# One-hot blocks as a stream of 22 a quad in the last two edge passes of a four-layer graph network

## The chip, the cores and the metric

The kernel runs on one core of one Trainium2 chip. The metric is the device time in microseconds of one execution; the kernel before has a median of 4281.43 us over 3 runs (4277.96 to 4282.35).

## The reference

The reference is a stack of four graph layers on 6250 nodes with 96 features each and 106250 edges, sorted by target. Each layer reads a row of some table for every edge (by its source node), reduces the rows over the edges of a target, adds the result to the nodes and normalizes. Cut to the third and fourth layer, which the change touches:

```python
# third layer: ci, cj from the degrees
msg = feat[src] * ci[src, None]
agg = segment_sum(msg, dst, N) * cj[:, None]
h = where(in_deg[:, None] > 0, agg, feat)
x = layernorm(x + h @ weight + bias)
# fourth layer
h = x @ W
agg = segment_sum(h[src] * edge_weight[:, None], dst, N)
y = agg + bias;  y = layernorm(y) * gamma + beta
x = layernorm(x + y)
```

## The kernel before

The edges are cut into 832 tiles of 128 edges and 208 quads of four tiles. Four passes run over the quads, one for each layer, with the nodes' own work between them and beside them. The nodes are 49 tiles of 128 (NT), in 13 chunks of four (NC). The engines are programmed by hand, each with its own queue in program order, and wait for each other through semaphores that count quads.

In the third and fourth pass a quad `q` goes through these steps:

- GpSimd (POOL) issues one indirect DMA for each tile (line L630), which gathers 128 rows of the table `ci_table` (third pass) or `h_table` (fourth) into `rows[:, q % 4]`. It waits for `agg_done` of quad q - 4, since `rows` holds four quads.
- VectorE (DVE) makes the one-hot matrices `same` from the targets' ranks: in the third pass by one comparison of 128x512 (`one_hot`, L1348), in the fourth by four operations of 128x128 that compare and multiply with the edge weight (L1696). It waits for `agg_done` of quad q - 2.
- TensorE (PE) adds the rows into their targets' window by four products, `spread` (L908, matmuls at L728), and counts `agg_done`.
- ScalarE (ACT) adds the window into the sums `acc` (the helper `spread` of ACT, L1028 to L1032).

Some tiles are not gathered by GpSimd but fetched by a product with a one-hot matrix. In the kernel before these are the last tiles of 60 quads in each pass (`picked`: every third quad from 18 to 195). Such a tile needs 49 blocks, one for each node tile: VectorE compares the 128 source numbers with the node numbers of a block (`find`, L1588, after `away`, L1583), TensorE multiplies each block with the table in `near` and `far`, kept in SBUF as three bf16 parts (`fetch`, L925, 128x288), and VectorE adds up the three parts into `rows` (`take`, L1595). The 49 blocks of a tile are dealt over the three quads before its own as 16, 16 and 17; `found` holds one tile's 49 blocks. The table's parts are made at the start of the pass by `make_exact` (L1565 to L1572), one chunk a quad, from `stage`, which SyncE loads (L596).

Side work on the 49 node tiles goes with the first 49 quads of each of these passes. In the third pass ScalarE and TensorE do it (L1205, L950, L958). In the fourth VectorE writes `x_plus` at the end of its quad (L1705, counts `v_plus`), and ScalarE's first step in the quad (L1243) waits for `v_plus` of that quad and counts `v_done`. The last twelve quads (from 196, `TAIL * GQ`) are left without fetched tiles.

## Time and profile before

| | us |
|---|---|
| median of 3 runs | 4281.43 |
| the profiled execution, its own time | 4278.2 |
| its span in the trace | 4276.2 |
| third pass, first to last gather's start | 2305.2 to 3268.8 |
| fourth pass, first to last gather's start | 3288.5 to 4254.8 |
| granted TensorE clock, mean | 0.843 |

The span runs from the first to the last instruction. Engines work side by side, so busy times don't add up to it; what counts is which engine never waits for another. A granted clock of 1 is the upper of TensorE's two levels (2.4 GHz), 0.5 the lower (1.2 GHz).

### The profile page before, as it was taken

How to read it: one execution, taken by the hardware profiler on the slowest of the kernel's cores; microseconds unless marked ns; L12 is line 12 of the kernel's file. 1: busy time of each engine (PE TensorE's matmuls, PEld its weight loads, DVE VectorE, ACT ScalarE, POOL GpSimd, SP SyncE). 2: the span in 40 equal slices, each digit the busy share in tenths (PEclk: the TensorE clock that was granted, in tenths of full speed). 3: DMA queues.
4: the chain of work that ended last, by engine and by line, in shares of the span. 5: the costliest groups of instructions: out<-in, count | busy, mean ns of one | idle time of the engine just before them, and what ended most of it. 6: DMA issues, size and time to landing. Idle time of an engine off the chain costs nothing.

```text
span 4276.2 us, 68563 instructions
## 1 busy us (share of the span) xinstructions
PE 3037.4 (71%) x20922; PEld 2603.9 (61%) x20922; DVE 2905.5 (68%) x5203; ACT 1377.3 (32%) x4318; POOL 3094.2 (72%) x3246
## 2 busy tenths in 40 slices
PE   7777777777666766676683787667775567776776
PEld 6677777777656666666662565555554455555555
DVE  4666666666676666666666566666665687777777
ACT  2222222222444444444454332222223222222223
POOL 5677777777277777777757777777776777777776
PEclk7777878777689888888895898999986699999997
DMA  7776776676443333333322222222222222222222
GB/s 216 202 188 178 188 187 182 182 188 179 105 121 100 100 98 100 100 100 98 100 74 62 49 45 45 45 45 45 45 44 67 55 45 44 45 45 46 44 45 56
DMA packets 363802, 417.49 MB, mean 98 GB/s; under 512 B 225184, under 2 KB 277011, under 8 KB 363357
## 3 DMA queue, kind: packets, MB, share of 16 engines
q0 software_dynamic: 129280, 239.67, 23.0%
q1 hardware_dynamic: 234173, 173.44, 15.2%
q8 instruction: 186, 3.05, 0.3%
q14 instruction: 163, 1.34, 0.1%
HBM read 393.05 MB, written 19.77 MB: 97 GB/s over the span
## 4 chain that ended last, share of the span: by engine, by line
POOL 61%; issue 21%; PE 8%; DMA 4%; DVE 3%; ACT 1%; SPq 1%; ACTq 0%; DVEq 0%; POOLq 0%
POOL rows L630 60%; PE bank L728 3%; DMA rows<-kv_table,src_idx 2%; DMA rows<-pair_table,src_idx 1%; PE bank L934 1%; POOL acc_max L657 1%; PE bank L825 1%; SPq L448 0%; PE bank L741 0%; PE bank L742 0%; PE bank L773 0%; PE bank L682 0%; DVE prod L1417 0%; DVE score L1419 0%; DVE prod L1415 0%
## 5 line engine op out<-in xcount | busy, mean ns | idle before, releaser
L728 PE MATMUL bank<-same,rows 128*96 128x128 f32 x4992 | 766.3, 304 | 364.8 <-issue 208.7
L630 POOL DMA_INDIRECT rows<-kv_table,src_idx x832 | 793.7, 954 | 314.1 <-issue 272.4
L630 POOL DMA_INDIRECT rows<-pair_table,src_idx x832 | 787.9, 947 | 311.5 <-issue 247.7
L728 PEld LDWEIGHTS bank<-same,rows 128*96 128x96 f32 x4992 | 658.7, 184 | 469.0 <-issue 407.8
L1030 ACT COPY acc<-bank 96x511 f32 (+1 forms) x832 | 480.1, 577 | 1365.8 <-PE bank L728 1364.6
L630 POOL DMA_INDIRECT rows<-h_table,src_idx x772 | 732.3, 949 | 253.7 <-issue 235.0
L630 POOL DMA_INDIRECT rows<-ci_table,src_idx x772 | 729.6, 945 | 243.3 <-issue 234.7
L1588 DVE TENSOR_TENSOR spare<-bank,first_only 128x2048 bf16<-128x2048 f32 x360 | 838.2, 2328 | 17.6
L925 PE MATMUL bank<-acc_max,spare 128*128 128x288 bf16 x4320 | 655.8, 307 | 164.8 <-DVE spare L1588 164.4
L925 PEld LDWEIGHTS bank<-acc_max,spare 128*128 128x128 bf16 x4320 | 437.6, 104 | 320.8 <-DVE spare L1588 194.1
L728 PE MATMUL bank<-same,msg 128*105 128x128 f32 x1664 | 307.6, 344 | 219.8 <-ACT acc L1032 219.5
L1348 DVE TENSOR_TENSOR same<-bank,rank_col 128x512 f32<-128x512 f32 x624 | 420.5, 674 | 41.8 <-PE bank L728 41.8
L741 PE MATMUL bank<-weights,first_only 97*128 97x96 f32 x1664 | 397.2, 329 | 33.3 <-DMA first_only<-q_table 29.6
L728 PEld LDWEIGHTS bank<-same,msg 128*105 128x105 f32 x1664 | 264.4, 225 | 239.8 <-DVE same L1348 174.1
L1487 DVE TENSOR_TENSOR_SCAN first_only<-first_only,bank 96x512 f32<-96x512 bf16 x208 | 264.7, 1273 | 199.4 <-issue 166.6
L742 PE MATMUL bank<-first_only 128*128 128x96 f32 x1664 | 399.0, 330 | 0.0
L825 PE MATMUL bank<-ident,rows 128*96 128x128 f32 x832 | 148.3, 307 | 305.9 <-DMA rows<-pair_table,src_idx 305.3
L741 PEld LDWEIGHTS bank<-weights,first_only 97*128 97x128 f32 x1664 | 335.1, 249 | 35.7 <-issue 35.6
L1595 DVE TENSOR_REDUCE rows<-bank 128x96 f32<-128x288 f32 x120 | 54.9, 457 | 430.2 <-PE bank L925 430.2
L742 PEld LDWEIGHTS bank<-first_only 128*128 128x128 f32 x1664 | 330.7, 246 | 0.0
L1415 DVE TENSOR_TENSOR prod<-bank,rows 128x384 f32<-128x384 f32 x208 | 115.6, 556 | 300.1 <-DMA rows<-kv_table,src_idx 235.1
L825 PEld LDWEIGHTS bank<-ident,rows 128*96 128x96 f32 x832 | 95.1, 138 | 346.1 <-DMA rows<-pair_table,src_idx 339.9
(184 smaller groups left out, 4172.6 us busy)
## 6 DMA issues: line engine op xcount, KB each, us to landing
first_only<-in_attr_cols SPq DMA_DIRECT2D x104, 384.0 KB, 4.1
first_only<-q_table SPq DMA_DIRECT2D x832, 48.0 KB
first_only<-rank_rows SPq DMA_DIRECT2D x104, 256.0 KB
first_only<-keep_rows SPq DMA_DIRECT2D x104, 192.0 KB, 3.2
rows<-kv_table,src_idx POOLq DMA_INDIRECT x832
rows<-pair_table,src_idx POOLq DMA_INDIRECT x832
rows<-ci_table,src_idx POOLq DMA_INDIRECT x772
rows<-h_table,src_idx POOLq DMA_INDIRECT x772
```

The source lines that it names most:

```text
L630: pool.indirect_dma_start(rows[:, k, j, 0:width], None, table, bass.IndirectOffsetOnAxis(ap=src_idx[:, t:t + 1], axis=0)).then_inc(rows_in ...
L728: mm = pe.matmul(out[0:nrow, here], left(j), right(j), start=(j == 0), stop=(j == TQ - 1), skip_group_check=True)
L741: pe.matmul(quad(bank[k % 2], F)[:, j, :], attr[:, k, j * P:(j + 1) * P], w_e, start=True, stop=True)
L742: mm = pe.matmul(quad(bank[2 + k % 2], F)[:, j, :], pick[:, k % 2, j * P:(j + 1) * P], q_win[:, k, j, :], start=True, stop=True)
L825: tr = pe.transpose(bank[k % 2][0:F, j * P:(j + 1) * P], rows[:, k, j, F:PAIR], ident[:])
L925: mm = pe.matmul(bank[0][:, 0:PARTS * F], found[:, t, :], exact(t)[:, 0, :], start=(t == 0), stop=(t == NT - 1), skip_group_check=True)
L1030: act.copy(dst[0:nrow, bass.ds(first + 1, QE - 1)], src[0:nrow, 1:QE])
L1348: return dve.tensor_tensor(out, base, over(values[:, bass.ds(q * TQ, TQ)], n), ALU.is_equal)
L1415: dve.tensor_tensor(prod[:], quad(bank[2 + k % 2], F), rows[:, k, :, 0:F], ALU.mult).then_inc(prod_step, 1)
L1487: dve.tensor_tensor_scan(scanned[:, k % 2, :], keep_row[:, k, :], bank[k % 2][0:F, :], 0.0 if static(q) and q == 0 else scanned[:, (k - 1) ...
L1588: dve.tensor_tensor(found[:, lo:hi, :], away.rearrange("p (o e) -> p o e", o=1).to_broadcast([P, hi - lo, P]), over(hundreds[:, lo:hi], P) ...
L1595: dve.tensor_reduce(rows[:, k, TQ - 1, 0:F], bank[0][:, 0:PARTS * F].rearrange("p (m f) -> p f m", m=PARTS), AX_X, ALU.add).then_inc(fetch ...
```

## The change

Both passes fetch 84 tiles in place of 60. The blocks are no longer dealt by thirds of a tile: from quad 5 on every quad up to 195 makes and uses the next 22 blocks of one long stream, across the borders of tiles. A tile's quad is the second one after that of its last block, so the fetched tiles lie in quads two or three apart. A quad whose 22 blocks cross a border does two pieces of `find`, with a new `away` between them; `away` and the PSUM bank of the products alternate between two. The rule for reuse of `found` becomes: the blocks of quad q wait until TensorE has used those of quad q - 2. `stage` has four buffers in place of two, and two chunks go through `make_exact` in each of the quads 1 to 7.

In the fourth pass, up to quad 195, the edge weight leaves the one-hot matrices: VectorE makes them by the same single comparison as in the third pass, and ScalarE multiplies the rows by the weight in place (`weigh`, four operations of 128x96). TensorE's `spread` now waits for `weighted` and not for the gathers. ScalarE's addition of quad q - 1 stands behind `weigh` of quad q.

```diff
-    EVERY = 3
     PARTS = 3
-    START = NC + 2 + EVERY
-    picked = list(range(START, TAIL * GQ, EVERY))
-    piece_of = [NT * m // EVERY for m in range(EVERY + 1)]
+    BLOCKS = 22
+    BEGIN = 5
+
+    def last_turn(g):
+
+        return BEGIN + ((g + 1) * NT - 1) // BLOCKS
+
+    picked = [last_turn(g) + 2 for g in range(NQ) if last_turn(g) + 2 < TAIL * GQ]
     order_of = {q: g for g, q in enumerate(picked)}
-
-    def piece(q):
-
-        for m in range(EVERY):
-            g = order_of.get(q + EVERY - m)
-            if g is not None:
-                return g, m
-        return None
+    pieces = [[] for _ in range(NQ)]
+    for q in range(BEGIN, TAIL * GQ):
+        lo, hi = (q - BEGIN) * BLOCKS, min((q - BEGIN + 1) * BLOCKS, len(picked) * NT)
+        while lo < hi:
+            end = min(hi, (lo // NT + 1) * NT)
+            pieces[q].append((lo // NT, lo % NT, end - lo // NT * NT))
+            lo = end
+    assert all(2 * (q - 1) * CT + 2 * CT >= min(NT, (q - BEGIN + 1) * BLOCKS) for q in range(BEGIN, BEGIN + 3))
+
+    def pieces_before(q):
+
+        return sum(len(pieces[p]) for p in range(max(q, 0)))
+
+    def pieces_through(g):
+
+        return sum(of <= g for p in pieces for of, _, _ in p)
...
-        stage = carve(2 * CT * F).rearrange("p (b t f) -> p b t f", b=2, t=CT)
+        stage = carve(4 * CT * F).rearrange("p (b t f) -> p b t f", b=4, t=CT)
...
-        away = bank[7][:, P:2 * P]
+        away = [bank[7][:, P:2 * P], bank[7][:, 256 + F:256 + F + P]]
...
-                wait(sp, staged, (n - 2) * NC + c - 1)
+                wait(sp, staged, (n - 2) * NC + c - 3)
                 m = len(tiles_of(c))
-                sp.dma_start(stage[:, c % 2, 0:m, :], rows_of(ci_table if n == 2 else h_table, c, 0, F)).then_inc(stage_in[c % 2].sem, 16)
+                sp.dma_start(stage[:, c % 4, 0:m, :], rows_of(ci_table if n == 2 else h_table, c, 0, F)).then_inc(stage_in[c % 4].sem, 16)
...
             def spread(s, q, i, k, at):
 
                 wait(pe, s.same_done, q + 1)
-                wait(pe, rows_in[k], arrivals(s.n, q))
-                if q in order_of:
-                    wait(pe, fetched, s.picks + order_of[q] + 1)
+                if s.n == 3 and q < TAIL * GQ:
+                    wait(pe, weighted, q + 1)
+                else:
+                    wait(pe, rows_in[k], arrivals(s.n, q))
+                    if q in order_of:
+                        wait(pe, fetched, s.picks + order_of[q] + 1)
                 wait(pe, s.copied, q - 1)
                 window(bank[2 + 2 * (k % 2)], F, at, lambda j: rows[:, k, j, 0:F], lambda j: same[:, k % 2, j, :]).then_inc(s.agg_done.sem, 1)
 
             def fetch(s, q):
 
-                at = piece(q)
-                if at is None:
-                    return
-                g, m = at
-                wait(pe, found_done, (s.picks + g) * EVERY + m + 1)
-                for t in range(piece_of[m], piece_of[m + 1]):
-                    mm = pe.matmul(bank[0][:, 0:PARTS * F], found[:, t, :], exact(t)[:, 0, :], start=(t == 0), stop=(t == NT - 1),
-                                   skip_group_check=True)
-                mm.then_inc(found_used.sem, 1)
+                n = s.pieces + pieces_before(q)
+                for g, lo, hi in pieces[q]:
+                    n += 1
+                    wait(pe, found_done, n)
+                    for t in range(lo, hi):
+                        mm = pe.matmul(bank[g % 2][:, 0:PARTS * F], found[:, t, :], exact(t)[:, 0, :], start=(t == 0), stop=(t == NT - 1),
+                                       skip_group_check=True)
+                    mm.then_inc(found_used.sem, 1)
...
+            def weigh(q, k):
+
+                wait(act, rows_in[k], arrivals(3, q))
+                if q in order_of:
+                    wait(act, fetched, s3.picks + order_of[q] + 1)
+                for j in range(TQ):
+                    at = q * TQ + j
+                    ins = act.mul(rows[:, k, j, 0:F], rows[:, k, j, 0:F], weight_col[:, at:at + 1])
+                ins.then_inc(weighted.sem, 1)
...
-                    spread(q, k, acc, F, bank[2 + 2 * (k % 2)], part_sum, s3.agg_done, s3.held, s3.copied)
+                    if q < TAIL * GQ:
+                        weigh(q, k)
+                    if 0 < q <= TAIL * GQ:
+                        spread3(q - 1, (k - 1) % GQ)
+                    if q >= TAIL * GQ:
+                        spread3(q, k)
...
             def find(s, q):
 
-                at = piece(q)
-                if at is None:
-                    return
-                g, m = at
-                if m == 0:
-                    wait(dve, src_in[g % 2], ((s.n - 2) * len(range(g % 2, len(picked), 2)) + g // 2 + 1) * 16)
-                    st.did(dve.tensor_scalar(away, src_row[:, g % 2, :], iota_col[:, 0:1], None, ALU.subtract))
-                    st.settle()
-                    dve.sem_inc(away_done.sem, 1)
-                lo, hi = piece_of[m], piece_of[m + 1]
-                wait(dve, found_used, (s.picks + g - 1) * EVERY + m + 1)
-                dve.tensor_tensor(found[:, lo:hi, :], away.rearrange("p (o e) -> p o e", o=1).to_broadcast([P, hi - lo, P]),
-                                  over(hundreds[:, lo:hi], P), ALU.is_equal).then_inc(found_done.sem, 1)
+                wait(dve, found_used, s.pieces + pieces_before(q - 1))
+                for g, lo, hi in pieces[q]:
+                    if lo == 0:
+                        wait(dve, src_in[g % 2], ((s.n - 2) * len(range(g % 2, len(picked), 2)) + g // 2 + 1) * 16)
+                        st.did(dve.tensor_scalar(away[g % 2], src_row[:, g % 2, :], iota_col[:, 0:1], None, ALU.subtract))
+                        st.settle()
+                        dve.sem_inc(away_done.sem, 1)
+                    dve.tensor_tensor(found[:, lo:hi, :], away[g % 2].rearrange("p (o e) -> p o e", o=1).to_broadcast([P, hi - lo, P]),
+                                      over(hundreds[:, lo:hi], P), ALU.is_equal).then_inc(found_done.sem, 1)
 
             def take(s, q, k):
 
-                n = s.picks + order_of[q]
-                wait(dve, found_used, (n + 1) * EVERY)
-                dve.tensor_reduce(rows[:, k, TQ - 1, 0:F], bank[0][:, 0:PARTS * F].rearrange("p (m f) -> p f m", m=PARTS), AX_X,
+                g = order_of[q]
+                wait(dve, found_used, s.pieces + pieces_through(g))
+                dve.tensor_reduce(rows[:, k, TQ - 1, 0:F], bank[g % 2][:, 0:PARTS * F].rearrange("p (m f) -> p f m", m=PARTS), AX_X,
                                   ALU.add).then_inc(fetched.sem, 1)
+
+            def make_two(s, q):
+
+                for c in (2 * q - 2, 2 * q - 1):
+                    if 0 <= c < NC:
+                        make_exact(s, c)
...
-                    for j in range(TQ):
-                        at = bass.ds(q * TQ + j, 1)
-                        ins = dve.tensor_scalar(same[:, k % 2, j, :], iota_s[:], rank_col[:, at], weight_col[:, at], ALU.is_equal, ALU.mult)
+                    if q < TAIL * GQ:
+                        ins = one_hot(same[:, k % 2], iota_over, rank_col, q, P)
+                    else:
+                        for j in range(TQ):
+                            at = bass.ds(q * TQ + j, 1)
+                            ins = dve.tensor_scalar(same[:, k % 2, j, :], iota_s[:], rank_col[:, at], weight_col[:, at], ALU.is_equal, ALU.mult)
                     ins.then_inc(s3.same_done.sem, 1)
                     if q in order_of:
                         take(s3, q, k)
-                    if 0 < q <= NC:
-                        make_exact(s3, q - 1)
-                    find(s3, q)
+                    make_two(s3, q)
+                    if pieces[q]:
```

The next two pieces are VectorE's queue in the fourth pass, in quads with side work (two quads between 21 and 25 in each). `acc_max<-spare` at L1705 or L1745 is the write of `x_plus`. Before:

```order
L1696 TENSOR_SCALAR same<-iota_s,rank_col,src_hi 128x128 [waits agg_done]
L1696 TENSOR_SCALAR same<-iota_s,rank_col,src_hi 128x128 x3
L1588 TENSOR_TENSOR spare<-bank,first_only 128x2176 [waits exp_done]
L1705 SCALAR_TENSOR_TENSOR acc_max<-spare,r_all,bank 128x96 [waits v_done]
L1696 TENSOR_SCALAR same<-iota_s,rank_col,src_hi 128x128 [waits agg_done]
L1696 TENSOR_SCALAR same<-iota_s,rank_col,src_hi 128x128 x3
L1595 TENSOR_REDUCE rows<-bank 128x96 [waits exp_done]
L1583 TENSOR_SCALAR bank<-first_only,iota_col 128x128 [waits rank_in1]
L1588 TENSOR_TENSOR spare<-bank,first_only 128x2048 [waits seq,exp_done]
L1705 SCALAR_TENSOR_TENSOR acc_max<-spare,r_all,bank 128x96 [waits v_done]
```

After:

```order
L1383 TENSOR_TENSOR same<-bank,rank_col 128x512 [waits agg_done]
L1626 TENSOR_REDUCE rows<-bank 128x96 [waits exp_done]
L1619 TENSOR_TENSOR spare<-bank,first_only 128x2304 [waits exp_done]
L1616 TENSOR_SCALAR bank<-first_only,iota_col 128x128 [waits rank_in0]
L1619 TENSOR_TENSOR spare<-bank,first_only 128x512 [waits seq]
L1745 SCALAR_TENSOR_TENSOR acc_max<-spare,r_all,bank 128x96 [waits v_done]
L1383 TENSOR_TENSOR same<-bank,rank_col 128x512 [waits agg_done]
L1619 TENSOR_TENSOR spare<-bank,first_only 128x2816 [waits exp_done]
L1745 SCALAR_TENSOR_TENSOR acc_max<-spare,r_all,bank 128x96 [waits v_done]
```

The four operations that make `same` have become one, `find` writes 2816 columns (22 blocks) in place of 2048 or 2176, and one of the quads cuts its 22 blocks in two (2304 and 512) around a new `away`.

ScalarE's queue, one quad of the same stretch. `x_nodes<-acc_max` is its share of the side work, `rows<-rows` is `weigh`. Before:

```order
L1243 ACTIVATE x_nodes<-acc_max,s_all 128x96 [waits v_plus]
L1025 TENSOR_LOAD starts
L1028 ISA [waits copied]
L1028 ACTIVATE part_sum<-acc,cont 96x1
L1030 ISA [waits agg_done]
L1030 COPY acc<-bank 96x511
L1032 ACTIVATE acc<-bank,part_sum 96x1 [waits held]
```

After:

```order
L1272 ACTIVATE x_nodes<-acc_max,s_all 128x96 [waits v_plus]
L1248 ACTIVATE rows<-rows,src_hi 128x96 [waits prod_done,rows_in2]
L1248 ACTIVATE rows<-rows,src_hi 128x96 x3
L1041 TENSOR_LOAD starts
L1044 ISA [waits copied]
L1044 ACTIVATE part_sum<-acc,cont 96x1
L1046 ISA [waits agg_done]
L1046 COPY acc<-bank 96x511
L1048 ACTIVATE acc<-bank,part_sum 96x1 [waits held]
```

The scalings stand between the side work, which waits for `v_plus`, and the addition to `acc`.

TensorE's queue in the fourth pass, a little later (`same,rows` is `spread`, the 128x288 products are `fetch`). Before:

```order
L728 MATMUL bank<-same,rows 96x128 [waits copied,rows_in2,same_done]
L728 ISA
L728 MATMUL bank<-same,rows 96x128
L728 ISA
L728 MATMUL bank<-same,rows 96x128
L728 ISA
L728 MATMUL bank<-same,rows 96x128
L925 MATMUL bank<-acc_max,spare 128x288 [waits clip_done]
L925 MATMUL bank<-acc_max,spare 128x288 x3
L925 MATMUL bank<-first_only,spare 128x288 x13
```

After:

```order
L742 MATMUL bank<-same,rows 96x128 [waits copied,pick_done,same_done]
L742 ISA
L742 MATMUL bank<-same,rows 96x128
L742 ISA
L742 MATMUL bank<-same,rows 96x128
L742 ISA
L742 MATMUL bank<-same,rows 96x128
L941 MATMUL bank<-first_only,spare 128x288 [waits clip_done]
L941 MATMUL bank<-acc_max,spare 128x288 [waits clip_done]
L941 MATMUL bank<-acc_max,spare 128x288 x20
```

`spread` waits for `pick_done` (the semaphore behind `weighted`) where it waited for the rows, and 22 products follow it in two pieces, where 17 did.

## Rows read from the trace of the kernel before

**Rows 1.** The page: busy time of each engine, and the chain that ended last, by engine.

```profile
PE 3037.4 (71%) x20922; PEld 2603.9 (61%) x20922; DVE 2905.5 (68%) x5203; ACT 1377.3 (32%) x4318; POOL 3094.2 (72%) x3246
...
POOL 61%; issue 21%; PE 8%; DMA 4%; DVE 3%; ACT 1%; SPq 1%; ACTq 0%; DVEq 0%; POOLq 0%
```

**Rows 2.** The gathers line L630: duration min/median/max in ns, first and last start; what ended its idle time.

```profile
L630 POOL DMA_INDIRECT rows<-ci_table,src_idx x772: 940/944/1292, 2305.2 to 3268.8; - x193
...
L630 POOL DMA_INDIRECT rows<-h_table,src_idx x772: 940/944/1302, 3288.5 to 4254.8; - x193
...
  issue: 989.7, 3150
...
  PE bank L728: 5.8, 19
```

**Rows 3.** Stretches: length, then busy (count) of PE, PEld, DVE, ACT, POOL; clock; DMA.

```profile
2500.00:3100.00 600.00, 441.46 (x3217) 338.15 (x3218) 407.96 (x350) 142.52 (x420) 453.72 (x481) 0.95 0.22 45
...
3500.00:4100.00 600.00, 440.04 (x3183) 333.88 (x3181) 466.23 (x747) 137.60 (x401) 453.72 (x481) 0.94 0.21 45
...
3289.00:3380.00 91.00, 38.06 (x164) 31.62 (x165) 52.99 (x141) 20.16 (x68) 69.36 (x72) 0.51 0.30 68
...
3380.00:3500.00 120.00, 86.88 (x636) 65.45 (x634) 95.54 (x169) 34.36 (x103) 90.75 (x97) 0.96 0.21 45
```

**Rows 4.** Timeline, third pass, quads without side work: start, length, instruction, [idle before].

```profile
2845.67 1.08 PE L728 MATMUL bank<-same,rows 128*96 128x128 f32 x8 [0.22 <-issue]
...
2845.97 0.68 DVE L1348 TENSOR_TENSOR same<-bank,rank_col 128x512 f32<-128x512 f32 x1
...
2846.57 2.41 DVE L1588 TENSOR_TENSOR spare<-bank,first_only 128x2176 bf16<-128x2176 f32 x1
...
2846.59 2.12 PE L925 MATMUL bank<-acc_max,spare 128*128 128x288 bf16 x16
...
2848.90 0.68 DVE L1348 TENSOR_TENSOR same<-bank,rank_col 128x512 f32<-128x512 f32 x1
```

**Rows 5.** Timeline, third pass, PE alone, a quad with side work.

```profile
2461.25 0.27 PE L950 MATMUL bank<-ident,acc_max 128*96 128x128 f32 x1
...
2462.23 0.49 PE L958 MATMUL bank<-rhs_u,acc_max 97*128 97x192 f32 x2
```

**Rows 6.** Timeline, fourth pass, DVE, PE and ACT in quads 36 to 38.

```profile
3467.64 0.46 DVE L1595 TENSOR_REDUCE rows<-bank 128x96 f32<-128x288 f32 x1 [2.33 <-PE bank L925]
...
3468.02 0.34 DVE L1583 TENSOR_SCALAR bank<-first_only,iota_col 128x128 f32<-128x128 int32 x1
...
3468.36 1.08 PE L728 MATMUL bank<-same,rows 128*96 128x128 f32 x8 [0.75 <-DVE rows L1595]
...
3468.51 2.29 DVE L1588 TENSOR_TENSOR spare<-bank,first_only 128x2048 bf16<-128x2048 f32 x1
...
3470.72 0.30 DVE L1705 SCALAR_TENSOR_TENSOR acc_max<-spare,r_all,bank 128x96 f32<-128x96 f32 x1
...
3470.94 1.11 DVE L1696 TENSOR_SCALAR same<-iota_s,rank_col,src_hi 128x128 f32<-128x128 f32 x4
...
3471.05 0.38 ACT L1243 ACTIVATE x_nodes<-acc_max,s_all 128x96 f32<-128x96 f32 x1 [4.67 <-DVE acc_max L1705]
...
3479.52 0.58 ACT L1030 COPY acc<-bank 96x511 f32 x1 [0.45 <-PE bank L728]
```

**Rows 7.** Timeline of POOL, fourth pass: first gather of quad 42.

```profile
3490.79 0.94 POOL L630 DMA_INDIRECT rows<-h_table,src_idx  x1 [0.30 <-issue]
```

**Rows 8.** Timeline of ACT: four scalings of 128x96 in a row.

```profile
3268.40 1.16 ACT L1197 ACTIVATE half<-spare,r_all 128x96 f32<-128x96 f32 x4
```

**Rows 9.** Timeline, start of the fourth pass: one call of make_exact and what follows.

```profile
3328.28 1.04 POOL L630 DMA_INDIRECT rows<-h_table,src_idx  x1 [0.30 <-issue]
...
3328.85 0.35 DVE L1565 CAST acc_max<-first_only 128x384 bf16<-128x384 f32 x1
...
3330.93 0.32 DVE L1705 SCALAR_TENSOR_TENSOR acc_max<-spare,r_all,bank 128x96 f32<-128x96 f32 x1
```

More of the change, by code:

```diff
@@ L1223, in _, with spread3 @@
             s3 = passes[3]
+            def weigh(q, k):
[6 more added lines that the diff above has]
+                ins.then_inc(weighted.sem, 1)
+            def spread3(q, k):
+                spread(q, k, acc, F, bank[2 + 2 * (k % 2)], part_sum, s3.agg_done, s3.held, s3.copied)
             def nodes5(slot):
@@ L1626, in third_pass @@
                         take(s2, q, k)
-                    if 0 < q <= NC:
-                        make_exact(s2, q - 1)
-                    find(s2, q)
+                    make_two(s2, q)
+                    if pieces[q]:
+                        find(s2, q)
                     if static(q):
@@ L1699, in fourth_pass @@
                         take(s3, q, k)
-                    if 0 < q <= NC:
-                        make_exact(s3, q - 1)
-                    find(s3, q)
+                    make_two(s3, q)
+                    if pieces[q]:
+                        find(s3, q)
                     if side_tile(q, kind):
```

9 lines of the change are left out of this document (6 added, 3 removed).

## The prediction

> **What bounds the kernel now.** I read the page first: GpSimd has the largest busy share but only 72%, and the chain that ended last is GpSimd for 61% and "issue" for 21% [rows 1]. The gathers' line shows what that means. In both passes a gather takes 944 ns in the median; in the whole kernel GpSimd stood idle 989.7 us for "issue", 3150 times, hence 0.31 us each, and only 5.8 us for TensorE [rows 2]. So it never really waits: 0.94 and 0.31 us make a step of 1.25 us from gather to gather. The stretches confirm it: 453.72 us busy at 0.944 us are 480.6 gathers in 600 us, 1.248 us each, and the figure is the same in the fourth pass, though VectorE is busy 466 us there and 408 us in the third [rows 3]. The passes' own ends agree: 963.6 us over 771 steps and 966.3 us over 771 [rows 2]. The reader is to see that these two passes last as long as GpSimd has gathers, and that the others have time left: TensorE 441 of 600 us, VectorE 408 and 466, ScalarE under 143 [rows 3].
>
> How far GpSimd is from waiting shows in the timeline. The addition of quad 38 starts at 3479.52, just after its `agg_done` [rows 6], and the gather that needs this signal, the first of quad 42, starts at 3490.79 [rows 7]: a lead of 11.3 us.
>
> **What it removes.** 24 gathers in each pass, 48 at 1.248 us: 59.9 us, if GpSimd goes on without a wait. The passes then have 748 gathers each. Between quads 5 and 195 a quad has 22/49 = 0.45 fetched tiles, hence 3.55 gathers or 4.43 us (before: 3.67 gathers, 4.58 us). The other engines must keep to 4.43 us a quad.
>
> **VectorE's queue.** From start to start, the comparison for `same` takes 0.60 us and 17 blocks take 2.33 us [rows 4]; 16 blocks take 2.21 [rows 6], so a block costs 0.12 to 0.13 us and a call 0.19. No row has 22 blocks; by these two, 22 take 2.21 + 6 x 0.127 = 2.97 us. From below it can't be less than 22/17 of the block part (2.33 - 0.19) and the call, 2.96; from above, 22/16 of the whole 2.21, 3.04. I take 2.97. `take` costs 0.38 us and `away` with its settling 0.49 (3467.64, 3468.02, 3468.51) [rows 6]. A quad comes to 0.60 + 2.97 + 0.45 x (0.38 + 0.49 + 0.19) = 4.05 us, under 4.43. In the fourth pass the four comparisons (1.11 us) [rows 6] give way to the one of 0.68 [rows 4]; without that VectorE would need 4.5 us and be the bound itself.
>
> **TensorE's queue.** `spread` takes 0.92 us from start to the next start (2845.67 to 2846.59), 16 products of `fetch` 2.12, of which the last lasts about 0.29, so 0.122 each [rows 4]; 22 take 2.69 to their last start. With the 0.2 us of idle before `spread`, 3.8 us a quad. In the third pass's first 49 quads come 0.11 us for the transpose (at 0.27 busy, mostly beside other work) and some 0.33 of the 0.49 us at L958 [rows 5]: 4.25 us, still under 4.43. I cost both queues at nothing in the third pass, and name GpSimd's gathers as the cover; it is thin, 0.2 to 0.4 us a quad.
>
> **The new wait in the fourth pass.** `weigh` is not in the trace; the nearest row is four scalings of the same size by a column, 1.16 us [rows 8]. From below its share on a path is nothing (ScalarE idles), from above four separate ones, 4 x 0.38 = 1.5 us by the side work's row [rows 6]. I take 1.16. In quads with side work ScalarE's queue has `weigh` of quad q behind the step that waits for `v_plus` of quad q, and VectorE writes `v_plus` after `find` of q. So TensorE's `spread` of q now waits for `find` of q, `fetch` of q stands behind it, and `find` of q + 2 waits for that `fetch`. Before, no such ring existed: `spread` needed the rows and `same` alone. Around the ring, for two quads: `find` 2.97; `x_plus` to ScalarE's start 0.33 (3470.72 to 3471.05); the side step 0.38; `weigh` 1.16; the last writer to TensorE 0.26 (end of `take` at 3468.10 to 3468.36) [rows 6]; `spread` 0.92 [rows 4]; 22 products to their end 2.85. Sum 8.87 us. Where the quad crosses a tile's border, and that is 77% of the hops in the parity that decides (49/22 = 2.23 quads from border to border, so two quads in 77 of 100 cases, else three), `take`, `away` and the second call add 1.06. Mean 9.69 us for two quads, 4.84 a quad against GpSimd's 4.43. Over quads 8 to 48, 41 of them, VectorE and TensorE fall behind by 41 x 0.41 = 16.8 us.
>
> Ahead of it is the start. One `make_exact` takes 2.08 us (3328.85 to 3330.93) [rows 9]. In quads 5 to 7 VectorE has two of them, `same`, 22 blocks and in the fourth pass `x_plus`: 4.16 + 0.60 + 2.97 + 0.30 = 8.0 us, while GpSimd needs 4.99; that is 9.1 us in three quads. In the third pass this is all, and GpSimd's lead of 11.3 us covers it. In the fourth it adds to the 16.8. The lead there is smaller by `weigh` and its signal (1.4 us), and by 0.4 us since the three quads ahead have fewer gathers: 9.5 us. So GpSimd waits 9.1 + 16.8 - 9.5 = 16.4 us. After quad 48 the ring is open and the queues get back their lead.
>
> **Sum.** -59.9 + 16.4 = -43.5 us on the profiled execution's 4278.2 us (span 4276.2, 2 us around it): 4234.7. The median of the runs is 3.2 us above that execution, so 4237.9 for the median; a little less stall is as likely as more, and I say 4237.
>
> **A rule that speaks against it.** Gathers beside `make_exact` take 1.04 us and not 0.94 (3328.28) [rows 9], those beside `find` 0.944 in the median [rows 2, 3]. The Trainium skill, page "SBUF — State Buffer", section "SBUF: two separate sides", says that VectorE and GpSimd contend for one pair of ports, and that a VectorE instruction with two SBUF inputs or in its faster mode shuts GpSimd out for its whole length; a gather's descriptors are then written late. By that rule more VectorE work costs gathers. The trace agrees for `make_exact`, whose number stays 13 a pass, and it shows nothing for `find`, whose operands lie in PSUM and SBUF; so the sum stays as it is.
>
> **Rivals.**
> - *The ring costs nothing* (27%): hops are shorter than their rows, since a wait that was idle before (0.26, 0.33) may overlap, and 0.4 us a quad is only 9% of the ring. If each hop is 0.8 us shorter, the stall is gone. Time 4281.4 - 59.9 = 4221.5. For it: VectorE's 4.05 and TensorE's 3.8 fit. Against: the ring has seven links, each from a row.
> - *The stall is larger* (20%): the clock. It is 0.94 to 0.96 while `fetch` runs and 0.51 before [rows 3], the lower level in a tenth of the time. At that level `spread` and `fetch`, 3.6 us, take 7.2. A tenth of 41 quads puts another 10 us on the ring at most; and in the third pass a TensorE quad of 4.25 us becomes 4.7 on the average, above 4.43, for 44 quads: 12 us less the lead left. Time 4246 to 4265.
> - *TensorE's clock decides, and the kernel is slower* (4%): TensorE at the lower level for long stretches, because its work is cut by waits for ScalarE and VectorE. A quad is 3.8 us at the upper level and 7.4 at the lower. The gain is gone when the 191 quads of a pass take 30 us more than by the gathers, 4.43 + 0.16 = 4.59 us each, hence with the lower level in 22% of the time; at 40% it is 5.24 us a quad, 0.65 x 382 = 248 us slower than before. Against: the level falls in the rows where TensorE has little to do, and it gets more.
> - *Gathers slow down under more VectorE work* (4%, half of it slower): 1496 gathers remain, so 0.040 us each would take the 59.9 us away; at 0.10 as beside `make_exact`, 90 us slower. Against: no change between the two passes at 408 and 466 us of VectorE.
> - My forecast, a stall of 8 to 24 us, has 45%: 4229 to 4246.
>
> **How the numbers follow.** 4221.5 with its run-to-run 2 us gives the lower end, 4219; the larger stall is taken in to 4258. About 0.2% or 8.6 us is what a measurement can tell from no change. All of the first three cases are faster: 92%. Within 0.2%: 2%. Slower: 4% and 2%, 6%.
>
> **What would show it.** Right: 748 gathers in each pass, a step of 1.248 us in the third pass throughout, first to last gather 933 to 936 us there; in the fourth 948 to 956 us, with GpSimd waiting for TensorE between quads 8 and 49 (waits of one to two microseconds, at a quad's first gather) and not after; `find` of 2816 columns at 3.05 us; four scalings at 1.16. TensorE's and VectorE's quads in the stretch of the ring at 4.84 us. Wrong: waits of GpSimd after quad 60, which would mean that a queue and not the ring is the bound; gathers longer than 0.95 us; or a clock below 0.9 while `fetch` runs.

## The result and the profile after

| | us |
|---|---|
| before, median of 4 runs beside it | 4279.86 (4277.96 to 4282.35) |
| after, median of 4 runs | 4216.82 (4215.77 to 4221.22) |
| ratio | 0.9855, 95% interval 0.9843 to 0.9867 |
| after, the profiled execution and its span | 4217.59, 4215.8 |

The changed kernel is 63.0 us or 1.5% faster. The prediction of 4237 had the direction, and the time lies 2.2 us under its lower end of 4219.

The page of the changed kernel, busy time and the chain by engine, answers to [rows 1]:

```profile
PE 3199.3 (76%) x23274; PEld 2782.4 (66%) x23274; DVE 3187.6 (76%) x4887; ACT 1564.6 (37%) x5102; POOL 3046.1 (72%) x3198
...
POOL 44%; issue 18%; PE 17%; DVE 13%; DMA 5%; ACT 1%; SPq 1%; ACTq 0%; DVEq 0%; POOLq 0%
```

VectorE and TensorE now have larger busy shares than GpSimd, and they have parts of the chain. That alone doesn't say that GpSimd waited for them. Its own line, now L644, says how long it did (it answers to [rows 2]):

```profile
L644 POOL DMA_INDIRECT rows<-ci_table,src_idx x748: 940/944/1288, 2302.8 to 3236.2; - x187
L644 POOL DMA_INDIRECT rows<-h_table,src_idx x748: 938/944/1326, 3255.6 to 4193.0; - x187
...
  issue: 955.4, 3035
...
  PE bank L742: 27.7, 85
```

The third pass lasts 933.4 us in place of 963.6, the fourth 937.4 in place of 966.3: together 59.1 us less, where 48 gathers at 1.248 are 59.9. The span is 60.4 us shorter; all else changed by little more than a microsecond in sum. A group "PE bank" of 27.7 us in 85 times looks like a wait for TensorE, but a gather has 0.305 us of idle before it (the median of the third and fourth pass) whatever stands beside it: 85 x 0.305 = 25.9 us are the usual step with another name on it, and 1.8 us are left as waiting. It lies before seven gathers of the fourth pass, the first ones of quads 36 to 46. One more idle time stands out, before the first gather of quad 52, and the trace names "issue" for it:

```profile
3495.04 0.94 POOL L644 DMA_INDIRECT rows<-h_table,src_idx  x1 [1.70 <-issue]
```

That is another 1.4 us above the usual step. Apart from the pass's very first, these eight are the only gathers in it with more than 0.34 us of idle before them (in the kernel before there is none), and together they hold 3.1 us above the usual step. That is the stall for which I forecast 16.4 us.

The stretches, which answer to [rows 3] (length, busy of PE, PEld, DVE, ACT, POOL, clock, DMA):

```profile
2500.00:2700.00 200.00, 172.64 (x1375) 137.98 (x1374) 180.90 (x150) 52.23 (x156) 151.23 (x161) 1.00 0.23 47
3259.00:3350.00 91.00, 56.03 (x396) 45.05 (x397) 79.60 (x113) 37.68 (x133) 69.06 (x72) 0.80 0.31 65
3350.00:3490.00 140.00, 115.85 (x921) 91.82 (x919) 130.34 (x134) 69.43 (x248) 104.39 (x112) 1.00 0.23 47
```

GpSimd makes 151.23 / 0.944 = 160 gathers in 200 us, a step of 1.248 as before. VectorE is busy 90% of the third pass and 93% of the ring's stretch. The granted clock is 1.00 where it was 0.94 to 0.96, and 0.80 in the first 91 us of the fourth pass, where it was 0.51.

The ring is there, in quads with side work of the fourth pass. The timeline of VectorE, ScalarE and TensorE shows a hop with a border, from one `find` to the `find` two quads later:

```profile
3400.95 1.62 DVE L1619 TENSOR_TENSOR spare<-bank,first_only 128x1408 bf16<-128x1408 f32 x1 [0.60 <-PE bank L941]
...
3402.50 0.34 DVE L1616 TENSOR_SCALAR bank<-first_only,iota_col 128x128 f32<-128x128 int32 x1
...
3402.99 1.62 DVE L1619 TENSOR_TENSOR spare<-bank,first_only 128x1408 bf16<-128x1408 f32 x1
...
3404.53 0.30 DVE L1745 SCALAR_TENSOR_TENSOR acc_max<-spare,r_all,bank 128x96 f32<-128x96 f32 x1
...
3404.87 0.38 ACT L1272 ACTIVATE x_nodes<-acc_max,s_all 128x96 f32<-128x96 f32 x1 [3.20 <-DVE acc_max L1745]
3405.15 1.15 ACT L1248 ACTIVATE rows<-rows,src_hi 128x96 f32<-128x96 f32 x4
3405.35 3.08 DVE L1619 TENSOR_TENSOR spare<-bank,first_only 128x2816 bf16<-128x2816 f32 x1
...
3406.41 1.08 PE L742 MATMUL bank<-same,rows 128*96 128x128 f32 x8 [1.67 <-DVE same L1383]
...
3407.33 1.51 PE L941 MATMUL bank<-first_only,spare 128*128 128x288 bf16 x11
...
3408.67 1.51 PE L941 MATMUL bank<-acc_max,spare 128*128 128x288 bf16 x11
...
3409.17 0.45 DVE L1626 TENSOR_REDUCE rows<-bank 128x96 f32<-128x288 f32 x1
...
3410.22 2.29 DVE L1619 TENSOR_TENSOR spare<-bank,first_only 128x2048 bf16<-128x2048 f32 x1 [0.60 <-PE bank L941]
```

This hop shows every link where the prediction had it: `find` in two pieces (3.58 us to L1745), 0.34 to ScalarE, 0.28 for the side step, 1.26 from the first scaling to `spread`, 0.92 to `fetch`, 2.85 to the end of the 22 products at 3410.18, and the next `find` at 3410.22. Sum 9.27 us; my terms gave 8.87 + 1.06 = 9.93. The reader is also to see `take` at 3409.17: it is done a microsecond before the products end, so its 0.38 us, which I had put into the ring, isn't in it.

How fast the ring runs on the whole is read from `spread`, TensorE's L742, at quads 4 to 6, at quad 8 and at quad 48:

```profile
3284.33 1.99 PE L742 MATMUL bank<-same,rows 128*96 128x128 f32 x8 [3.61 <-issue]
...
3292.31 1.99 PE L742 MATMUL bank<-same,rows 128*96 128x128 f32 x8 [5.99 <-DVE same L1383]
...
3300.32 1.08 PE L742 MATMUL bank<-same,rows 128*96 128x128 f32 x8 [2.80 <-DVE same L1383]
...
3309.73 1.08 PE L742 MATMUL bank<-same,rows 128*96 128x128 f32 x8
...
3492.24 1.08 PE L742 MATMUL bank<-same,rows 128*96 128x128 f32 x8
```

From quad 8 to 48 it is 182.51 us for 40 quads, 4.56 a quad against my 4.84 and GpSimd's 4.43: 5.3 us lost, not 16.8. From one `spread` to the one two quads later it is mostly 9.26 or 9.27 us with a border and 8.70 to 8.78 without.

### The profile page after: what moved, and what is told of

Read it like the earlier page. It is cut to its first block, busy times and chain, and to the rows that moved or that the text cites. A ratio compares the mean times of both kernels' runs of the same rounds, so it can differ in the third digit from the quotient of the medians.

```text
span 4215.8 us, 73837 instructions
## 1 busy us (share of the span) xinstructions
PE 3199.3 (76%) x23274; PEld 2782.4 (66%) x23274; DVE 3187.6 (76%) x4887; ACT 1564.6 (37%) x5102; POOL 3046.1 (72%) x3198
## 4 chain that ended last, share of the span: by engine, by line
POOL 44%; issue 18%; PE 17%; DVE 13%; DMA 5%; ACT 1%; SPq 1%; ACTq 0%; DVEq 0%; POOLq 0%
POOL rows L644 43%; DVE spare L1619 7%; PE bank L941 7%; PE bank L742 6%; DMA rows<-kv_table,src_idx 2%; DVE same L1383 2%; DMA rows<-pair_table,src_idx 1%; PE bank L950 1%; POOL acc_max L671 1%; PE bank L755 1%; PE bank L756 1%; SPq L462 0%; PE bank L839 0%; DVE prod L1452 0%; DVE score L1454 0%
## 5 line engine op out<-in xcount | busy, mean ns | idle before, releaser
L1619 DVE TENSOR_TENSOR spare<-bank,first_only 128x2816 bf16<-128x2816 f32 (+14 forms) x536 | 1180.7, 2203 | 130.3 <-PE bank L941 103.7
L644 POOL DMA_INDIRECT rows<-kv_table,src_idx x832 | 793.8, 954 | 310.6 <-issue 271.3
L644 POOL DMA_INDIRECT rows<-pair_table,src_idx x832 | 787.3, 946 | 309.5 <-issue 248.6
L742 PE MATMUL bank<-same,rows 128*96 128x128 f32 x4992 | 747.8, 298 | 312.7 <-issue 184.4
L742 PEld LDWEIGHTS bank<-same,rows 128*96 128x96 f32 x4992 | 642.1, 180 | 413.9 <-issue 281.4
L644 POOL DMA_INDIRECT rows<-h_table,src_idx x748 | 707.6, 946 | 249.2 <-issue 208.0
L644 POOL DMA_INDIRECT rows<-ci_table,src_idx x748 | 706.7, 945 | 236.0 <-issue 227.4
L941 PE MATMUL bank<-acc_max,spare 128*128 128x288 bf16 x6048 | 814.5, 286 | 2.4 <-DVE spare L1619 2.3
L941 PEld LDWEIGHTS bank<-acc_max,spare 128*128 128x128 bf16 x6048 | 591.9, 98 | 146.5 <-DVE spare L1619 4.8
L1383 DVE TENSOR_TENSOR same<-bank,rank_col 128x512 f32<-128x512 f32 x820 | 554.9, 677 | 30.8 <-PE bank L742 30.5
L742 PE MATMUL bank<-same,msg 128*105 128x128 f32 x1664 | 308.9, 345 | 214.2 <-ACT acc L1048 214.1
L742 PEld LDWEIGHTS bank<-same,msg 128*105 128x105 f32 x1664 | 265.2, 226 | 234.3 <-DVE same L1383 167.0
L1248 ACT ACTIVATE rows<-rows,src_hi 128x96 f32<-128x96 f32 x784 | 228.7, 362 | 368.3 <-DMA rows<-h_table,src_idx 355.1
```

What stands on the lines that cost most here:

```text
L644: pool.indirect_dma_start(rows[:, k, j, 0:width], None, table, bass.IndirectOffsetOnAxis(ap=src_idx[:, t:t + 1], axis=0)).then_inc(rows_in ...
L742: mm = pe.matmul(out[0:nrow, here], left(j), right(j), start=(j == 0), stop=(j == TQ - 1), skip_group_check=True)
L941: mm = pe.matmul(bank[g % 2][:, 0:PARTS * F], found[:, t, :], exact(t)[:, 0, :], start=(t == 0), stop=(t == NT - 1), skip_group_check=True)
L1248: ins = act.mul(rows[:, k, j, 0:F], rows[:, k, j, 0:F], weight_col[:, at:at + 1])
L1383: return dve.tensor_tensor(out, base, over(values[:, bass.ds(q * TQ, TQ)], n), ALU.is_equal)
L1619: dve.tensor_tensor(found[:, lo:hi, :], away[g % 2].rearrange("p (o e) -> p o e", o=1).to_broadcast([P, hi - lo, P]), over(hundreds[:, lo: ...
```

## The experiments

Two theories stood against each other at first. **Ring:** VectorE, ScalarE and TensorE depend on each other in a ring, that ring is slower than GpSimd in quads 8 to 48, and it only happens to cost little because the lead pays for it. **No ring:** the engines' queues alone count, and the new wait costs nothing by itself. Of every run I read the fourth pass from first to last gather, since first passes of one and the same code differ by 5 us and more from run to run (1071 to 1080 us here), which is larger than most of what is asked.

**1. Open the ring.** The scalings go ahead of ScalarE's side work, so that they no longer wait for `v_plus`.

```diff
+                    if q < TAIL * GQ:
+                        weigh(q, k)
...
-                    if q < TAIL * GQ:
-                        weigh(q, k)
```

> weigh ahead of the side step, repeated, since on the chip of the first four runs every engine stood still for some 1.7 us about every 10 us, the kernel before included (5229 us). Ring theory as before: quads 8 to 48 of the fourth pass at 4.43 us with a lead of GpSimd that stays over 4 us, 1 us shorter than the changed kernel, 4215 to 4220 us on a chip like the first. Rival, VectorE's queue alone: 4.56 us a quad, lead down to 0.3 us.

4218.06 us (4211.43 to 4220.45), ratio 0.9865 (0.9848 to 0.9881) to its own kernel before (4277.98). By the total this is no different from the change. GpSimd's line:

```profile
L644 POOL DMA_INDIRECT rows<-h_table,src_idx x748: 940/944/1292, 3254.5 to 4188.9; - x187
...
  PE bank L742: 29.5, 94
```

934.4 us against 937.4, and no gather of the pass has more than 0.34 us of idle before it, that of quad 52 included. The smallest lead (from the end of `spread` of quad q to the first gather of quad q + 4) is 6.7 us in quads 8 to 100; in the changed kernel it goes down to 0.27 us, which is GpSimd waiting. So the ring ate the whole lead and then cost 3 us: the 3.1 us of waits above are gone with it, and the pass is shorter by as much. That it cost so little is the finding against my number, not against the ring.

**2. Make the ring longer.** Four more operations of 128x96 into an unused tile ahead of the scalings, 0.69 us from start to start, so `weigh` takes 1.84 us in place of 1.15.

```diff
             def weigh(q, k):
...
+                for j in range(TQ):
+                    act.mul(msg[:, k % 2, j, 0:F], rows[:, k, j, 0:F], 1.0)
                 for j in range(TQ):
```

> weigh twice as long, repeated for the same reason. Ring theory: 5.14 us a quad in quads 8 to 48, GpSimd waits some 25 us for TensorE there, the kernel is 20 to 28 us slower than the changed one: 4238 to 4246 us. Rival, VectorE's queue alone: 0 to 1 us slower.

4238.53 us (4235.56 to 4241.24), ratio 0.9909 (0.9893 to 0.9926). GpSimd's line and two of its gathers in the timeline:

```profile
L644 POOL DMA_INDIRECT rows<-h_table,src_idx x748: 938/944/1292, 3259.9 to 4215.3; - x187
...
  PE bank L742: 32.7, 54
```

```profile
3397.96 0.94 POOL L644 DMA_INDIRECT rows<-h_table,src_idx  x1 [0.95 <-PE bank L742]
...
3407.35 0.94 POOL L644 DMA_INDIRECT rows<-h_table,src_idx  x1 [0.95 <-PE bank L742]
```

The fourth pass is 955.4 us, 18.0 longer. 32.7 - 54 x 0.305 = 16.2 us are waits for TensorE, at a quad's first gather and all of them at or before quad 51; two more idle times, at quads 23 and 52, have the name "issue" and hold 4.1 us. Together they are 20.4 us against 3.1. I had expected some 25, with 1.15 us more in each hop where 0.69 were added; a quad of the ring takes 4.96 us. ScalarE is busy 1699 of 4238 us in this kernel, so its own queue isn't full; 0.69 us matter because they stand in the ring.

**3. Both together.** The longer scalings, but ahead of the side work. If the extra time counts as work, it costs the same here; if it counts as a link of the ring, it costs nothing.

> weigh twice as long but ahead of the side step, repeated. Ring theory: fourth pass within 2 us of 934.4 us. Rival, a longer path from the rows to agg_done or a busier ScalarE costs by itself: over 940 us.

4221.78 us (4213.86 to 4227.62), ratio 0.9853 (0.9838 to 0.9868), fourth pass 934.7 us. The cost is gone: this parts the theories, and "no ring" falls. The rival of a ScalarE that is simply too busy falls too, for its work is the same in both runs. The changed kernel ran again beside it:

> The changed kernel once more, beside the variants. The two passes that changed gave 30.2 and 28.9 us less from first to last gather; if the rest of the difference is scatter of the first two passes, the difference of the medians comes out at 58 to 62 us, and the passes at 933.4 and 937.5 us as before.

It had 4229.85 us (4216.79 to 4233.06), ratio 0.987 (0.9855 to 0.9885), with the kernel before at 4287.55: 57.7 us less, just under the 58 to 62 expected. The passes are 933.8 and 937.4 us, and the first gather of quad 52 has 1.72 us of idle before it again, named "issue". In all the waits of the fourth pass are 2.2 us here.

**4. Leave the scalings out.** The fourth pass goes back to four comparisons with the weight on VectorE; the stream of 22 blocks stays.

```diff
-                if s.n == 3 and q < TAIL * GQ:
-                    wait(pe, weighted, q + 1)
...
-                    if q < TAIL * GQ:
-                        weigh(q, k)
...
-                    if q < TAIL * GQ:
-                        ins = one_hot(same[:, k % 2], iota_over, rank_col, q, P)
```

> The stream of 22 blocks with the edge weight back in VectorE's four comparisons of the fourth pass, and no weigh on ScalarE: one part of the change undone. VectorE's quad is then 0.43 us longer, 4.47 us in the mean after quad 48 and 4.71 before, against the gathers' 4.43. If VectorE's queue binds: 41 x 0.28 = 11.5 us, 147 x 0.04 = 6 us and 7 us of the start, less a lead of 11 us, so the fourth pass is 10 to 16 us longer than the changed kernel's, 4227 to 4233 us. If the weighing in the changed kernel is what costs (the ring), undoing it gives time back: 4216 us or less.

4229.68 us (4226.09 to 4233.29), ratio 0.989 (0.9873 to 0.9906), and the fourth pass 941.6 us, 4.2 longer than in the changed kernel where I had expected 10 to 16. (The total fell into the expected range only because the passes that the edit leaves alone were longer too.) In the stretch of this pass from 3330 to 3460:

```profile
3330.00:3460.00 130.00, 106.26 (x842) 84.44 (x840) 128.09 (x205) 35.39 (x109) 98.36 (x104) 0.99 0.24 47
```

VectorE is busy 128.09 of 130 us: it is the bound, at 4.67 us a quad up to quad 48 and 4.45 after. The lead shrinks slowly and is used up before quad 49. But the waits are only 4.3 us against 3.1. The other 3.0 of the 4.2 us are gathers that take longer: 30 of them last over 0.98 us, against 10 in the changed kernel. Twelve of the 30 lie beside `make_exact`. What such gathers cost scatters between 0.8 and 3.3 us a pass in the runs here, and it is 1.6 us more in this run. The other 18 lie beside the four comparisons, like this one:

```profile
3426.92 1.11 DVE L1729 TENSOR_SCALAR same<-iota_s,rank_col,src_hi 128x128 f32<-128x128 f32 x4
...
3427.79 1.06 POOL L644 DMA_INDIRECT rows<-h_table,src_idx  x1 [0.30 <-issue]
```

The kernel before shows the same: 40 such gathers in its fourth pass, 19 of them beside L1696 without `make_exact`, and none of the 419 gathers that touch neither. Above the usual 0.944 us the gathers beside comparisons hold 1.4 us here, 1.7 in the kernel before and 0.2 in the changed one, which has comparisons in the last twelve quads only. So taking the weight off VectorE pays 1.2 us in waits and 1.2 us in gathers; the rest of the 4.2 is scatter. The second 1.2 I hadn't seen.

**5. More blocks.** If GpSimd still sets the time, 24 blocks a quad (92 fetched tiles, 8 gathers fewer a pass) give 10 us a pass; if the ring is near, the fourth pass gets nothing from it.

```diff
-    BLOCKS = 22
+    BLOCKS = 24
```

> 24 blocks a quad in place of 22: 93 or so fetched tiles a pass. If GpSimd's gathers still set the pace, some 18 gathers fewer at 1.248 us: 20 to 22 us faster than the changed kernel. VectorE's quad becomes 4.04 + 0.25 + 0.04 = 4.33 us against 4.38 of the gathers, and with side work and the ring 4.9: in quads 8 to 48 of the fourth pass 41 x 0.5 = 20 us and 7 us of the start less a lead of 11 us are lost. Ring theory: net 3 to 8 us faster than the changed kernel, 4209 to 4214 us. Rival, VectorE's queue alone (4.57 us with side work): 41 x 0.19 = 8 us, hidden by half, net 18 us faster.

4217.61 us (4211.64 to 4219.58), ratio 0.9863 (0.9847 to 0.988): nothing gained in all, where I had expected 3 to 8 us. The passes tell why:

```profile
L644 POOL DMA_INDIRECT rows<-ci_table,src_idx x740: 940/944/1292, 2301.4 to 3226.7; - x185
L644 POOL DMA_INDIRECT rows<-h_table,src_idx x740: 938/944/1287, 3246.1 to 4188.2; - x185
...
  PE bank L742: 47.0, 95
```

The third pass became 8.1 us shorter, the fourth 4.6 longer, with 47.0 - 95 x 0.305 = 18.0 us of waits for TensorE. The 3.5 us that are left are less than the scatter of the first pass. Two more blocks make a hop of the ring, by my estimate, 0.5 us longer (a block in `find` and one in `fetch`, 0.12 to 0.13 each, twice).

**6. More blocks with the ring open.**

> 24 blocks a quad with weigh ahead of the side step, repeated, since every engine stood still now and then on the chip of the last runs. Ring theory: the 15 us of waits of the run with 24 blocks in quads 20 to 48 of the fourth pass are gone, fourth pass 926 to 930 us in place of 942, the kernel 4200 to 4206 us. Rival, VectorE is simply full at 24 blocks: the fourth pass stays over 938 us.

4206.31 us (4201.7 to 4213.26), ratio 0.9818 (0.9805 to 0.9832), 0.56% under the changed kernel on the same chip (4229.85):

```profile
L644 POOL DMA_INDIRECT rows<-ci_table,src_idx x740: 940/944/1292, 2307.6 to 3232.1; - x185
L644 POOL DMA_INDIRECT rows<-h_table,src_idx x740: 938/944/1289, 3251.8 to 4177.7; - x185
...
  PE bank L742: 16.0, 46
```

The fourth pass is 925.9 us, 16.1 less than in experiment 5 by the order of two calls alone. This is the best of the kernels that ran. What comes next shows in its stretches too:

```profile
3700.00:3900.00 200.00, 183.05 (x1490) 149.02 (x1489) 196.62 (x160) 91.64 (x329) 151.23 (x161) 1.00 0.24 48
```

VectorE has 3.4 us of 200 left: it is about to take GpSimd's place as the bound. Up to quad 48 it has done so already: a quad takes 4.55 us with the ring open, more than the gathers, and GpSimd waits 16.0 - 46 x 0.305 = 2.0 us.

**7. The start.** The stream begins at quad 9, after the last `make_exact` (83 fetched tiles), to see what the start lag is worth.

```diff
-    BEGIN = 5
+    BEGIN = 9
```

> The stream begins at quad 9, repeated. Theory of the start: the lead at quad 8 is 10 us or more in place of 3.8, the ring takes 5 us of it by quad 49, GpSimd never waits; fourth pass 936 to 937 us. If the lead still falls to 0.3 us, the start is not what mattered.

4227.8 us in one run. The lead at quad 8 is 10.4 us where the changed kernel has 3.8, GpSimd waits no more (28.7 us in 94 times, the plain step), the smallest lead in quads 20 to 49 is 1.3 us, and the fourth pass is 936.6 us, all as expected. The third pass is 938.8 us, where I expected 934.7: every gather lasted 0.003 us longer in this run (median 947 ns), which is 2.2 us a pass, and 13 gathers over 0.98 us, 12 of them beside `make_exact`, add some 2 us more than the 6 of the changed kernel. One run doesn't tell this kernel from the change beside it (4229.85).

**The same kernels on a chip that stops.** In two sets of runs the kernel before took 5229.08 and 5218.48 us, and the variants 5088 to 5151 us. The changed kernel in the first of them:

> The changed kernel once more, on the chip that the variants below share. If the 60.4 us between the two profiled spans are 59.0 us of the two passes and the rest is scatter of the first two passes, this run gives 4217 to 4221 us and a difference of 58 to 63 us; a steady 63 us would mean that something outside the two passes has gained.

```profile
L644 POOL DMA_INDIRECT rows<-h_table,src_idx x748: 938/945/1290, 3980.2 to 5121.6; - x187
...
  remote: 514.1, 264
...
  PE bank L742: 178.3, 108
```

```profile
3300.32 1.76 PE L941 MATMUL bank<-first_only,spare 128*128 128x288 bf16 x13
...
3301.33 3.09 DVE L1619 TENSOR_TENSOR spare<-bank,first_only 128x2816 bf16<-128x2816 f32 x1 [2.18 <-remote]
3301.50 0.58 ACT L1046 COPY acc<-bank 96x511 f32 x1 [7.58 <-remote]
3301.65 0.94 POOL L644 DMA_INDIRECT rows<-ci_table,src_idx  x1 [1.94 <-remote]
...
3311.79 0.69 DVE L1619 TENSOR_TENSOR spare<-bank,first_only 128x512 bf16<-128x512 f32 x1 [2.82 <-remote]
...
3312.12 0.94 POOL L644 DMA_INDIRECT rows<-ci_table,src_idx  x1 [2.02 <-remote]
```

VectorE, ScalarE and GpSimd start nothing for nearly 2 us and go on together, here 10.47 us apart; GpSimd was idle 514 us in 264 such times. TensorE doesn't always stop with them: the 13 products above run on at their usual 0.122 us, and it is busy in 58% of such idle time of GpSimd in the third and fourth pass. So "every engine stood still", as I wrote in some expectations, says too much. The gathers last as long as elsewhere (945 ns in the median). Here the lead is short, and a ring costs more:

> ScalarE does weigh of a quad before its side step, which waits for v_plus. Ring theory: in quads 8 to 48 of the fourth pass the hop over VectorE, ScalarE, TensorE is what makes 4.56 us a quad; with the ring open the quads fall to VectorE's own 3.82 and 4.85 us, 4.28 in the mean, below the gathers' 4.43, so GpSimd keeps a lead of 5 us or more and the fourth pass is 1 us shorter (936.4 us from first to last gather). Rival, VectorE's queue alone: still 4.56 us a quad and the same lead lost down to 0.3 us; no change in time.

> weigh is twice as long: four more scalings of 128x96 by 1 into an unused tile stand before it. Ring theory: each hop is 1.15 us longer, 10.4 us with a border and 9.8 without, 5.14 us a quad, so quads 8 to 48 fall behind by 29 us, with the 6 us of the start and a lead of 9.7 us some 25 us of waits of GpSimd; the kernel is 20 to 28 us slower than the changed one, all of it before quad 49 of the fourth pass. Rival, VectorE's queue alone: 0 to 1 us slower, since VectorE has no more to do.

> The doubled weigh of the run before, but ahead of the side step. Ring theory: nothing of the 25 us is left, within 2 us of the changed kernel. Rival, ScalarE is simply too busy with the doubled weigh: as slow as the run before.

| first such chip, before 5229.08 us | us | ratio (95%) | fourth pass |
|---|---|---|---|
| the change | 5139.36 | 0.9822 (0.9798 to 0.9846) | 1141.4 |
| ring open | 5113.87 | 0.9792 (0.9773 to 0.9811) | 1119.3 |
| longer scalings | 5151.18 | 0.9863 (0.984 to 0.9885) | 1152.3 |
| both | 5112.91 | 0.978 (0.9759 to 0.9802) | 1123.3 |

Opening the ring gives 22 us in the fourth pass here, where it gave 3 on an undisturbed chip, and the pattern of experiments 1 to 3 is the same. In the second set (before 5218.48):

> The changed kernel once more, for a closer ratio and the scatter of the first two passes. The two passes that changed gave 30.2 and 28.9 us less from first to last gather; the rest of the 60.4 us between the profiled spans stood before the third pass (2.4 us) or between and behind the passes. If that rest is scatter, the difference of the medians comes out at 58 to 62 us.

> 24 blocks a quad with weigh ahead of the side step. Ring theory: the 15 us of waits of the run with 24 blocks in quads 20 to 48 of the fourth pass came from the ring (4.85 us a quad); with the ring open VectorE's own 4.33 and 0.25 us of side work remain against 4.38 of the gathers, so quads 8 to 48 lose 41 x 0.2 = 8 us of a lead of 7 to 10 us, and GpSimd waits 0 to 3 us. Fourth pass 926 to 930 us from first to last gather in place of 942, the kernel 4200 to 4206 us. Rival, VectorE is simply full at 24 blocks: the fourth pass stays over 938 us.

> weigh twice as long but ahead of the side step, repeated on an undisturbed chip. Ring theory: the 18 us of the doubled weigh in the fourth pass are gone, first to last gather within 2 us of 934.4. Rival, a longer path from the rows to agg_done or a busier ScalarE costs by itself: over 940 us.

> The stream begins at quad 9, after the table's parts are made, in place of quad 5; 83 fetched tiles for 84 (one gather more a pass, 1.25 us). Theory of the start: quads 5 to 7 need VectorE twice, which costs some 6 us of the lead in the fourth pass; without that the lead at quad 8 is 10 us or more in place of 3.8, the ring takes 5 us of it by quad 49, and GpSimd never waits. Fourth pass 936 to 937 us from first to last gather, third pass 934.7, the kernel within 2 us of the changed one. If the lead still falls to 0.3 us, the ring takes more than 0.13 us a quad and the start is not what mattered.

The change had 5119.64 us, 0.9818 (0.9794 to 0.9843); 24 blocks with the ring open 5087.69, 0.9753 (0.973 to 0.9776); both edits of experiment 3 5100.46, 0.9778 (0.9753 to 0.9803); the stream from quad 9 5104.97 in one run. The order is that of the other chips, with wider distances. The cause of the stops isn't known. They don't go with a chip's number: the record has number 8 for the first of these sets and also for the runs of experiments 3, 6 and 7, which have none.

## Why the prediction was right in direction and wrong in size

- **What bounds the kernel** was right: 748 gathers a pass, 944 ns in the median, a step of 1.248 us throughout. The forecast of the third pass was 933 to 936 us, and it is 933.4; the 29.95 us of its 24 gathers came in as 30.2.
- **The queues** were right to a few hundredths: `find` of 2816 columns lasts 3.08 us (3.05 forecast), four scalings 1.15 or 1.16 (1.16), `fetch` of 22 products 2.85. GpSimd's cover held in the third pass, where no gather waited.
- **The step that failed** is the one of the new wait and what was set against it: "So GpSimd waits 9.1 + 16.8 - 9.5 = 16.4 us." The ring is real (experiments 1, 2, 3 and 6), but it cost 3.1 us. Each of the three numbers erred to the same side:
  - the ring, 16.8: it measured 5.3. The hop with a border is 9.27 us and not 9.93. `take` (0.38) isn't in it; the side step is 0.28 from start to start, and I had used its whole duration, 0.38; from ScalarE's last scaling to TensorE it is 0.10 us, and I had taken 0.26 from another pair of engines in [rows 6]. The excess over GpSimd was 0.41 us a quad, a small difference of large sums, so an error of 6% in the hops took away two thirds of it. Most of that error is in the border's price: 9.27 against 8.70 to 8.78 us are 0.5 us, where I had added 1.06.
  - the start, 9.1: it measured about 6.6. Two quads take 7.98 and 8.01 us from one `spread` to the next, as forecast, but the third has one `make_exact` with one node tile in it (49 = 12 x 4 + 1) where I counted two full ones, and takes 5.58 us. With GpSimd at 4.99 a quad that is 21.57 - 14.97. Experiment 7 takes the start away, and with it all waits.
  - the lead, 9.5: it measured 10.9 at quad 4, and 3.8 at quad 7. I had taken both the scalings and the shorter quads off a lead read at quad 38, far from where it is used.
  With these the same sum gives 6.6 + 5.3 - 10.9 = 1.0 us; taken from the leads themselves, of which the last 0.3 can't be used, it is 5.3 - (3.8 - 0.3) = 1.8 us, which is what the trace puts down to TensorE. The other 1.4 us, at quad 52, are in no term. They appear where the lead is short (the change, its repeat, experiments 2 and 4) and not with the ring open in experiments 1 and 3; what makes them is not shown. The mechanism was right, the size wrong by 13 us.
- **The clock** was given only as a risk (20%). It went the other way: the granted clock was 1.00 in the stretches above in place of 0.95, and no part of the ring's stretch from 3350 on was at the lower level.
- **Gathers beside `find`** are as long as before, 944 ns, with VectorE busy 90%. By the rule on the shared ports in the Trainium skill (page "SBUF — State Buffer", section "SBUF: two separate sides"), a VectorE instruction with two SBUF inputs or in its faster mode keeps GpSimd out while it runs. The trace agrees for `make_exact`, beside which 8 of the 10 gathers over 0.98 us lie. What I overlooked is that gathers were stretched beside the fourth pass's four comparisons too (19 of 40 before, see experiment 4), which have one SBUF input; whether they ran in a faster mode no row tells. The change took most of these comparisons away. Shorter gathers gave 2.0 us which the sum had at nothing, 1.5 of them by the comparisons: the fourth pass became 28.9 us shorter, which is 29.95 of gathers and 2.0 of shorter ones, less 3.1 of waits.
- **The range.** The case "the ring costs nothing" had 27%, and it came nearest, at 4221.5 by its own sum. I gave it 2 us below, while the first pass alone scatters by 5 and more. The profiled execution before stood 3.2 us under its median, the one after 0.8 above: those 4.0 us, 15.6 us in the two passes (13.3 of waits that didn't come, 2.0 of shorter gathers, 0.3 in the third pass), and 1.5 us elsewhere in the span and around it are the 21.1 us from the sum's 4237.9 to 4216.8.

## What to carry to other kernels

A wait that closes a ring over several engines is priced by the ring's whole length against the pace of the slowest engine outside it, and only once the lead is used up; lengthen one link by a known amount, then the same with the ring open, and the two runs tell a ring from a full queue. Where a term is a small difference of two large sums (0.41 of 4.8 us), the error of the sums is the range: carry it through, and take links from start to start, not from durations. Before adding work to a stream, look for the order of calls that opens the ring: here two lines moved made room for 8 more fetched tiles a pass.

## What the runs showed of the hardware

- GpSimd's idle before a gather is 0.305 us in the median even where the trace names TensorE as its releaser; such a row is a wait only by what it has above that. And a wait can stand under "issue": 1.70 us at quad 52.
- A gather beside a 128x128 comparison from SBUF into SBUF on VectorE can take 0.98 to 1.07 us in place of 0.944 (19 of 327 gathers before, 18 of 338 in experiment 4); beside `find` alone, which reads PSUM too, none of the fourth pass's did.
- TensorE got more to do and lost no clock by it: granted 0.94 to 0.96 in the passes before [rows 3] and 1.00 after (1 is 2.4 GHz), and at the start of the fourth pass 0.51 and 0.80. Over the whole kernel it is 0.836 to 0.847 in the runs of the kernel before and 0.860 to 0.869 in those of the change, outside the two sets with stops.
- In two sets of runs VectorE, ScalarE and GpSimd stopped together for about 2 us at a time, once in 10.5 us in the rows above, and TensorE worked on in 58% of that time. The kernel before was 22% longer there; that the stops made it so is likely and not shown, as its own trace from there isn't kept.
